# Where the expert tiles run: two batches beside attention, or one stage between the two layers

## The reference

```python
x = x + tanh(g_xattn[0]) * L0_xattn(ctx, layernorm(x), mask, ...)   # 8 heads of 64
x = x + tanh(g_ffn[0])   * L0_ffn(layernorm(x), gate_w, w1, w2, w3) # 8 experts, top 2
x = x + tanh(g_xattn[1]) * L1_xattn(ctx, layernorm(x), mask, ...)   # 16 heads of 64
x = x + tanh(g_ffn[1])   * L1_ffn(layernorm(x), w1, conv_w, conv_b, w2)
...
y   = w2[e] @ (silu(w1[e] @ t) * (w3[e] @ t))      # for each of a token's two experts
out = sum of y over the two experts, weighted by the sparse mixer of their logits
```

## Time and profile before

| what | us |
|---|---|
| median of three runs | 1522.95 |
| the three runs | 1511.71 to 1533.22 |
| the profiled execution | 1511.2 |
| its span, first to last instruction | 1509.4 |

### The profile page before, as it was taken

One profiled execution on the slowest core, in us unless ns is written; L12 is line 12 of the kernel. 1 busy time (PEld: TensorE's weight loads), 2 busy tenths in 40 slices (PEclk: granted clock), 3 DMA queues, 4 the chain that ended last, 5 costly groups with the idle time before them and its releaser, 6 DMA issues.

```text
span 1509.4 us, 45217 instructions
## 1 busy us (share of the span) xinstructions
PE 1266.7 (84%) x16918; PEld 992.1 (66%) x16918; DVE 1055.9 (70%) x2830; ACT 973.3 (64%) x2319; POOL 1112.8 (74%) x1359
## 2 busy tenths in 40 slices
PE   1777788668879889868999999999999999999952
PEld 1445566447658767646888888677777777776742
DVE  4778788976556556775666666678878778777744
ACT  2678787455446566645656565777778777787831
POOL 5778888696567675457676777788888988888764
PEclk9999999889989999989999999999999999999965
DMA  9599998495998974448999998455455456355520
GB/s 313 138 204 237 252 237 186 75 232 141 249 204 235 230 161 84 95 98 196 240 247 255 251 261 221 93 102 107 92 98 101 100 103 106 87 104 99 79 41 7
DMA packets 438329, 239.96 MB, mean 159 GB/s; under 512 B 388848, under 2 KB 420320, under 8 KB 429024
## 3 DMA queue, kind: packets, MB, share of 16 engines
q1 hardware_dynamic: 408216, 178.51, 57.6%
q10 hardware_dynamic: 26824, 51.22, 11.2%
q0 software_dynamic: 3072, 7.34, 1.8%
HBM read 107.78 MB, written 35.50 MB: 95 GB/s over the span
## 4 chain that ended last, share of the span: by engine, by line
PE 23%; POOL 17%; ACT 16%; DMA 12%; DVE 12%; issue 9%; DVEq 4%; SPq 3%; ACTq 3%; POOLq 0%
POOL probs L649 5%; PE bank_ring L1128 5%; DMA probs_turned<-probs 5%; DMA expert_up<-experts_up 5%; ACT scores L844 4%; PE bank_ring L1090 4%; ACT probs L851 4%; DVE scores L1344 4%; PE bank_ring L1076 3%; PE bank_ring L1143 2%; DMA context<-in_ctx 2%; ACTq L987 2%; ACT keys L864 2%; ACT values L871 2%; PE bank_out L1109 2%
## 5 line engine op out<-in xcount | busy, mean ns | idle before, releaser
L649 POOL TENSOR_TENSOR probs<-scores,probs 112x487 f16<-112x487 f32 x384 | 424.9, 1123 | 207.7 <-ACT probs L851 202.1
L844 ACT ACTIVATE scores<-scores,score_min 112x487 f32<-112x487 f32 x384 | 265.9, 694 | 146.0 <-DVE score_min L1344 144.4
L1361 DVE SCALAR_TENSOR_TENSOR values<-bank_ring,values 128x512 f16<-128x512 f32 x192 | 132.4, 690 | 207.8 <-ACT values L871 207.3
L1344 DVE CUSTOM_DVE_ANT_0 scores<-bank_scores,mask 112x487 f32<-112x487 f32 x384 | 238.2, 657 | 1.8 <-PE bank_scores L1049 1.8
L851 ACT ACTIVATE probs<-scores 112x487 f16<-112x487 f32 x384 | 214.6, 604 | 33.0 <-DMA probs_turned<-probs 17.7
L1090 PE MATMUL bank_ring<-weights,kv_B 128*128 128x128 f16 x3072 | 194.9, 220 | 0.9 <-DVE raw_weights L1639 0.6
L1090 PEld LDWEIGHTS bank_ring<-weights,kv_B 128*128 128x128 f16 x3072 | 183.2, 99 | 11.5 <-DVE raw_weights L1639 0.9
L1109 PE MATMUL bank_out<-values,probs_turned 128*128 128x64 f16 x4608 | 170.4, 194 | 23.3 <-DMA probs_turned<-probs 20.8
L1076 PE MATMUL bank_ring<-kv_B,weights 128*128 128x488 f16 x768 | 181.9, 373 | 9.3 <-DVE keys L1356 9.2
L871 ACT ACTIVATE values<-bank_ring 128x512 f16<-128x512 f32 x192 | 112.2, 584 | 100.4 <-PE bank_out L1109 96.3
L1109 PEld LDWEIGHTS bank_out<-values,probs_turned 128*128 128x128 f16 x4608 | 157.2, 99 | 28.0 <-DMA probs_turned<-probs 14.1
(11 more groups left out here) (230 smaller groups left out, 2479.4 us busy)
## 6 DMA issues: line engine op xcount, KB each, us to landing
expert_up<-experts_up SPq DMA_DIRECT2D x43, 1024.0 KB, 5.3
expert_down<-experts_down SPq DMA_DIRECT2D x43, 512.0 KB, 6.8
raw_weights<-in_weights ACTq DMA_DIRECT2D x8, 1536.0 KB, 11.1
experts_up<-expert_up ACTq DMA_DIRECT2D x8, 1024.0 KB, 5.0
raw_weights<-in_weights ACTq DMA_DIRECT2D x6, 1024.0 KB, 8.9
probs_turned<-probs SPq DMA_TRANSPOSE x384
context_turned_B<-kv_B ACTq DMA_DIRECT2D x16, 375.0 KB, 8.5
kv_B<-context_turned_B ACTq DMA_DIRECT2D x16, 375.0 KB, 3.7
```

The source lines that it names most:

```text
L649: pool.tensor_tensor(PR[:, u % 4, 1, 0:KEYS], S[:, u % 4, 0:KEYS], PR[:, u % 4, 0, 0:KEYS], ALU.subtract).then_inc(probs_split, 1)
L844: act_e.activation(S[:, u % 4, 0:KEYS], S[:, u % 4, 0:KEYS], ACT.Exp, bias=rmin[:, u % 4:u % 4 + 1], scale=-1.0, accum_out=rsum[:, g % 2, ...
L1344: dve.tensor_tensor_reduce(out=S[:, u % 4, 0:KEYS], in0=bS[u % 2][0:TOK, 0:KEYS], in1=mask[:, m, 0:KEYS], scale=1.0, scalar=3.0e38, op0=AL ...
L1361: dve.scalar_tensor_tensor(vN[:, j % 2, 1].rearrange("p t d -> p (t d)"), bank("v", j)[:], 1 / WSCALE, vN[:, j % 2, 0].rearrange("p t d -> ...
```

## The change

The steps of layer B no longer follow those of layer A: `pair(s)` maps steps 0 to 63 to layer A and steps from `B_STEP` = 120 to layer B. Between them, from `FIRST_TILE` = 75, one stage runs all tiles, one a step. Routing goes in four groups of sequences (0 to 4, 5 to 9, 10 to 13, 14 and 15); the state `room`, `end` and `pages` carries over from group to group, so a group's rows first fill what is free on an expert's last page and then open new ones. As all groups share pages, there are at most 35 tiles. Each group's choices follow its last sequence, and its rows are scattered two a step; experts and weights of the choices are worked out once, from step 77. Rows of a tile are loaded plainly and turned by PE (`turn_rows`, four transposes) and copied by ACT (`copy_rows`), not by a DMA transpose; weights have three buffers, the third in the place of layer A's attention weights; `down` of a tile runs two steps behind its `up`. Expert chunks are prepared one a step, steps 1 to 48; the FFN weights are summed and rounded from steps 52 and 58 on, layer B's weights split from step 67. The diff, cut:

```diff
 PAIRS = A_STEPS + 8 * NSEQ
-FIRST_STEP, LAST_STEP = -9, PAIRS + 21
+
+
+GROUPS = ((0, 5), (5, 10), (10, 14), (14, 16))
+TILES = (2 * TOK * NSEQ + EXPERTS * 127) // 128
+SCATTERS = 2
+XR_SLOTS = 8
+ZERO_DMAS = -(-TILES // XR_SLOTS)
+
+
+def slack(g):
+    return 0 if g == NSEQ - 1 else 1
+
+
+def routed(b):
+    n = GROUPS[b][1] - 1
+    return 4 * n + 10 + slack(n)
+
+
+FIRST_TILE = routed(len(GROUPS) - 1) + 5
+DOWN_LAG = 2
+B_STEP = FIRST_TILE + TILES + DOWN_LAG + 8
+FIRST_STEP, LAST_STEP = -9, B_STEP + 8 * NSEQ + 21
 PT_BUFS = 5
 
 
-BATCHES = ((0, 6), (6, 16))
-TILES = tuple((2 * TOK * (b - a) + EXPERTS * 127) // 128 for a, b in BATCHES)
-SCATTERS = (3, 4)
-XR_SLOTS = 10
-ZERO_DMAS = sum(-(-t // XR_SLOTS) for t in TILES)
-
-
-def is_pair(j):
-    return 0 <= j < PAIRS
+def pair(s):
+
+    if 0 <= s < A_STEPS:
+        return s
+    return s - B_STEP + A_STEPS if B_STEP <= s < B_STEP + PAIRS - A_STEPS else None
+
+
...
-def first_tile_step(b):
-    return routed(b) + 4 + -(-len(scatters(b)) // SCATTERS[b])
-
-
-def tile(b, i):
-    return i + (TILES[0] if b else 0)
-
...
+def tile_up(s):
+    i = s - FIRST_TILE
+    return i if 0 <= i < TILES else None
+
+
+def tile_turn(s):
+    return tile_up(s + 1)
+
+
+def tile_down(s):
+    return tile_up(s - DOWN_LAG)
 
...
 
 EXPERT_STEP = 1
-WSUM_STEP = 31
-FFN_SUM_STEP, FFN_STEP = 26, 32
-L1_STEP = 41
+FFN_SUM_STEP, WSUM_STEP, FFN_STEP = 52, 57, 58
+L1_STEP = FFN_STEP + 9
+WEIGH_STEP = FIRST_TILE + 2
 
 
 def expert_chunks(j):
-    i = 2 * (j - EXPERT_STEP)
-    return range(i, i + 2) if 0 <= i < EXPERTS * MOE_CHUNKS else range(0)
+    i = j - EXPERT_STEP
+    return range(i, i + 1) if 0 <= i < EXPERTS * MOE_CHUNKS else range(0)
...
         if is_pair(j):
-            uses.append(("v", j))
-        if m[1]:
-            uses.append(m[1])
+            uses.append(("v", pair(j)))
+        if tile_up(j) is not None:
+            uses.append(("up", tile_up(j), 1))
+        if tile_down(j) is not None:
+            uses.append(("down", tile_down(j)))
         uses += late(j)
-        if m[2]:
-            uses.append(m[2])
     return uses
...
+        ctx_flat = ctxb[:].rearrange("p a t d -> p (a t d)")
+        aT = ctx_flat.bitcast(F16).rearrange("p (b a m t) -> p b a m t", b=3, a=2, m=EB)
+        tile_ups = [eup[:, 0], eup[:, 1], W[:, 0:UP_WORDS]]
+        tile_downs = [edown[:, 0], edown[:, 1], W[:, UP_WORDS:UP_WORDS + DOWN_WORDS]]
...
+            def load_rows(t):
+                if t == 0:
+                    for b in range(len(GROUPS)):
+                        sp.wait_ge(scattered[b], 16 * len(scatters(b)))
                 if t >= 2:
-                    sp.wait_ge(up_ready, 2 * (t - 2) + 2)
-                sp.dma_start_transpose(xT[:, t % 2], xs[b][128 * i:128 * i + 128, :])\
-                    .then_inc(xt_loaded[t % 2], 16)
...
+            def load_up(t):
+                if t == 0:
+                    sp.wait_ge(slots_ready, len(GROUPS))
                     sp.wait_ge(ex_stored[0], 32 * 4)
                     sp.wait_ge(ex_stored[1], 32 * 4)
-                e = sp.value_load(ids[b][0:1, i:i + 1], min_val=0, max_val=EXPERTS - 1)
-                if part == 0:
-                    if t >= 2:
-                        sp.wait_ge(up_ready, 2 * (t - 2) + 2)
...
-                else:
-                    if t >= 2:
-                        sp.wait_ge(down_ready, t - 1)
-                    sp.dma_start(edown[:, t % 2], down_dram[e]).then_inc(down_loaded[t % 2], 16)
-
-            def store_result(b, i):
...
+            def load_down(t):
+                e = sp.value_load(ids[0:1, t:t + 1], min_val=0, max_val=EXPERTS - 1)
+                if t >= 3:
+                    sp.wait_ge(down_ready, t - 2)
+                sp.dma_start(tile_downs[t % 3], down_dram[e]).then_inc(down_loaded[t % 3], 16)
+
+            def store_result(t):
                 sp.wait_ge(down_copied, t + 1)
-                sp.dma_start(ys[b][128 * i:128 * i + 128, :], yo[:, t % 2]).then_inc(y_stored[t % 2], 16)
...
-                        load_expert(b, i + 1, 0)
-                    if 2 <= i < TILES[b]:
-                        load_expert(b, i, 1)
+                if j == FIRST_TILE - 2:
+                    load_up(0)
+                    load_down(0)
+                    load_rows(0)
+                    load_rows(1)
+                    for t in (1, 2):
+                        load_up(t)
+                        load_down(t)
+                i = tile_up(j)
+                if i is not None:
+                    if i + 2 < TILES:
+                        load_rows(i + 2)
+                    if i + 3 < TILES:
+                        load_up(i + 3)
+                if 2 <= j - FIRST_TILE and j - FIRST_TILE + 1 < TILES:
+                    load_down(j - FIRST_TILE + 1)
+                if tile_down(j) is not None:
+                    store_result(tile_down(j))
                 for n in range(NSEQ):
...
                         scatter(b, n, k)
+                if tile_up(j) is not None:
+                    split_hidden(tile_up(j), 0)
...
+            def copy_rows(t):
+                act_e.wait_ge(rows_turned, t + 1)
+                if t >= 2:
+                    act_e.wait_ge(up_ready, 2 * (t - 2) + 2)
+                act_e.activation(xT[:, t % 2], bank("rows", t)[:].bitcast(F16)[:, 0:512]
+                                 .rearrange("p (k t) -> p k t", k=4), ACT.Copy).then_inc(rows_copied, 1)
+
...
+            def turn_rows(t):
+                ring_free("rows", t)
+                pe.wait_ge(rows_loaded[t % 2], 16 * (t // 2 + 1))
+                bT = bank("rows", t)[:].bitcast(F16)
+                for q in range(4):
+                    last = pe.transpose(bT[:, 128 * q:128 * q + 128], rows_in[:, t % 2, 128 * q:128 * q + 128], idh[:])
+                last.then_inc(rows_turned, 1)
...
-                m = micro(j)
-                expert(m[0])
+                    proj_q(p)
+                    proj_k(p)
+                if tile_up(j) is not None:
+                    up(tile_up(j), 0)
+                if tile_turn(j) is not None:
+                    turn_rows(tile_turn(j))
                 for t in early(j):
                     part(t)
                 if is_pair(j):
-                    proj_v(j)
-                expert(m[1])
+                    proj_v(pair(j))
+                if tile_up(j) is not None:
+                    up(tile_up(j), 1)
+                if tile_down(j) is not None:
+                    down(tile_down(j))
                 if is_pair(j - 2):
-                    sum_values(j - 2)
...
+            def choose_slots(b, i):
+                n0, n1 = GROUPS[b]
                 nb = n1 - n0
                 lg = LG[:, n0:n1]
...
                 src, top, place = (t2 if i else lg), rv[:, i], rv[:, 2 + i]
                 dve.tensor_reduce(top[:, 0:nb], src, AX.X, ALU.max)
                 dve.drain()
                 dve.tensor_tensor(t1, src, spread(top, nb), ALU.is_equal)
-                dve.tensor_tensor(ex, lg, spread(top, nb), ALU.subtract)
-                dve.scalar_tensor_tensor(keep, lg, -1.0, spread(top, nb), ALU.mult, ALU.max)
                 dve.drain()
                 dve.tensor_tensor(t1, t1, every, ALU.mult)
-                dve.tensor_scalar(ex, ex, 0.0, None, ALU.min)
-                dve.tensor_tensor(keep, keep, lg, ALU.max)
                 dve.drain()
                 dve.tensor_reduce(place[:, 0:nb], t1, AX.X, ALU.max)
-                last = dve.scalar_tensor_tensor(keep, keep, JITTER, ex, ALU.mult, ALU.add)
-                if i:
-                    last.then_inc(route_shifted, 1)
                 dve.drain()
                 dve.tensor_tensor(one[i], t1, spread(place, nb), ALU.is_equal)
...
-                n0, n1 = BATCHES[b]
-                nb, nt = n1 - n0, TILES[b]
+                n0, n1 = GROUPS[b]
+                nb = n1 - n0
                 t1, t2 = rt["t1"][:, 0:nb], rt["t2"][:, 0:nb]
...
                 dve.wait_ge(side_filled, SIDE_AT[("route", b)])
-                dve.tensor_copy(t1, bX[0:TOK, 0:nb * EXPERTS].rearrange("p (n e) -> p n e", e=EXPERTS))
...
+                dve.tensor_scalar(tmp, new, ROUND, None, ALU.add)
+                dve.drain()
+                dve.tensor_scalar(new, tmp, ROUND, None, ALU.subtract)
+                dve.drain()
+                dve.tensor_tensor(c8[:], lower[:],
+                                  new.rearrange("p (o e) -> p o e", o=1).to_broadcast([128, EXPERTS, EXPERTS]),
                                   ALU.mult)
...
-                dve.tensor_tensor(t1, t1, each[0:TOK].rearrange("p (o e) -> p o e", o=1)
-                                  .to_broadcast([TOK, nb, EXPERTS]), ALU.add)
-                dve.tensor_tensor(cmp_[:, 0:nt],
-                                  tile_no[:, 0:nt].rearrange("p (t o) -> p t o", o=1).to_broadcast([128, nt, EXPERTS]),
-                                  ends.rearrange("p (o e) -> p o e", o=1).to_broadcast([128, nt, EXPERTS]),
```

(43 more changed lines are left out.)

411 lines of the change are left out of this document (194 added, 217 removed).

## The result

The changed kernel takes 1570.22 us (1559.89 to 1579.49, four runs), the kernel before on the same chip 1528.09 us (1511.71 to 1536.81, four runs): a ratio of 1.031, 95% interval 1.019 to 1.043. It is slower, by 1.9 to 4.3%, about the 42 us between the medians; forecast was no change, 1530 us in a range from 1495 to 1570. The profiled execution took 1571.77 us with a span of 1570.0 us.

What follows compares the result with a forecast made beforehand. It took PE to bound layer B and no engine alone layer A. Terms 50.9 + 443.2 + 233.5 + 726.6 + 62.6 = 1516.8 us, 7.4 above the 1509.4 span; added to the 1522.95 median, 1530, range 1495 to 1570.

Steps and rivals of the forecast that it cites:

- a tile takes 4.7 us: Stage between the layers: each tile 4.7 us, between bounds of 4.3 and 5.9; 35 tiles make 164.5 us.
- Both lower bounds: Tiles of the stage: PE's work 4.3 us a tile; transport of 1.84 MB at 427 GB/s also 4.3 us.
- the new waits: Stage: SP's first rows wait for scatters, PE's turn of rows for their load, POOL's first gather for the last store.
- rival 1: Stage: tiles wait for their weights, 5.9 us a tile, +42 us, 1572 us; chance 0.26 with whatever else lengthens the stage.
- 8 us of waits for transposes in layer A: Layer A: waits like the 9.74 us one come with expert loads and stores, whose number stays; 8 in all.
- The forecast's own sign: Layer A: the forecast is wrong if a step leaves 5.7 to 7.1 us.
- 6.4 us a step: Layer A, steps 0 to 55: one chunk a step gives 6.4 us each, 358.4 us in all.
- two routings at 13: Layer A: two groups of five sequences routed inside its steps, 13 us extra each, 26 in all.
- Entry: Start of the stage, before the tiles: 40 us, plus 5 for the third group's place_rows ahead of norm_out.
- exit with the last downs: End of the stage: 4 us for the last two downs and 20 us from result copy to first mask.
- 37 us for eight tiles fewer: Whole kernel: 35 tiles instead of 43 earn 37 us of some 199 if nothing else moved.
- Rival 3: Whole kernel: nothing fuses, stage and layers cancel within 2%; this is the forecast itself, chance 0.58.

Runs made afterwards that it cites:

- e_noload: The changed kernel without the loads of the weights of experts 2 to 7, stores kept: 1549.78 us, one execution.
- the four traces: Traces with the same layer A code: the changed kernel, e_rows, e_rows_half, and the changed kernel with 6 of 35 tiles run; layer A 458.7 to 472.7 us.
- e_groups3: The changed kernel with three groups of sequences instead of four and three scatters a step instead of two: 1557.81 us, ratio 1.024 to the kernel before.
- b_35: The kernel before with 15 and 20 tiles run instead of 18 and 25, all result stores kept: 1482.83 us, one execution.
- b_few: The kernel before with 2 + 2 of its 43 tiles run, all result stores kept: 1351.09 us.
- the repaired forms: Three versions of the changed kernel with early rows, chunkwise expert weights and three groups, differing in groups, scatters and result buffers: each at ratio 0.997 to the kernel before.
- e_rows: The changed kernel with a tile's rows loaded six tiles ahead instead of two: 1531.76 us, ratio 1.013 to the kernel before.
- e_rows_half: e_rows with only half of each weight load made from tile 3 on: 1520.9 us in one execution.
- e_all2: The changed kernel with early rows, chunkwise expert weights, groups of 7, 6 and 3 sequences and two scatters a step: 1507.71 us, ratio 0.997 to the kernel before.

## Why the prediction was wrong

**Forecast: a tile takes 4.7 us. Measured: a pitch of 5.61, and 193.5 us where the term had 164.5.** This is the largest error, 29 us. Both lower bounds were nearly right: PE's 4.3 is 4.21 measured, and with early rows, where the transport holds the tiles, its 4.3 by the earlier trace rows has become 4.48. The step that failed is "Two loops of equal length never mesh fully; I take 4.7". There were not two loops but a chain through both, from one load of rows to another, and it has its own length, 11.0 us for two tiles: 4.2 of work and issues, and 6.8 for a load that is asked for behind 1.5 MB. The forecast had this wait in its hand twice. Under the new waits it names PE's turn of the rows, with `up` and `down` behind, and gives it no time; and rival 1 names the queue, with a chance of 0.26 together with whatever else lengthens the stage. That rival 1's 1572 us are close to the 1570 measured is partly luck: it put all 42 us on the tiles, at 5.9 us for lack of bandwidth. The bandwidth was there, the tiles brought 29 us, and layer A, which it left as forecast, 22.

The Trainium skill's 358 GB/s a core ("DMA: Bandwidth & Descriptors", Specifications) would have made an estimated 5.1 us a tile. The stage with early rows moved 405 GB/s, of which 1.70 of every 1.84 MB, 374 GB/s, are reads. The measurement decides against it as a limit here. The Trainium skill's 81 ns for each weight load and matmul ("TensorE: Matmul & The Clock Gate", Back-to-back issue gap) would have added an estimated 1.2 us to PE's part of a tile, 5.5 in all. It is 4.21.

**Forecast: 8 us of waits for transposes in layer A. Measured: 19 to 33 us hang on the loads of expert weights** (e_noload against the four traces; 26.0 against the changed kernel's). The term was sized from the single wait of 9.74 us in the earlier trace rows, with the argument that the number of loads stays. What failed is that step: the number stayed, but where a load, a store and a context's spill came together one or two transposes held all for 10 to 28 us. The forecast's own sign showed it, a step of layer A above 7.1 us: steps 8 to 23 took 7.6. The rest of layer A was right: 6.4 us a step (6.26 in e_noload); two routings at 13 (steps 27 to 30 take 38.0 us and 47 to 50 39.1, 12.4 and 13.5 over 6.4 each); the last eight steps 46.2 against 50.8. Some 9 us of steps 0 to 55 (419.4 less 358.4, 25.9 and 26.0) went away in no run; in e_noload 4.6 of them are step 33. Nor was one chunk a step the relief that the forecast took it for: without tiles, layer A is as long in the one form as in the other.

**Entry 47.6 against 45, exit with the last downs 26.9 against 24.** Near, but the third group's routing on DVE delays norm_out by 7.1 us (e_groups3) where place_rows had been given 5.

**Layer B 723.9 against 726.6, tail 62.6.** Right.

**37 us for eight tiles fewer.** Right in size: 28.4 to 34.4 us in b_35. A tile beside attention costs 4.1 to 4.3 us rather than the 4.6 of 199/43.

**Why the change loses,** all by the spans of the traces: eight tiles fewer at the 4.1 us of b_few -33; the other 35 at 5.53 us in the stage (193.5/35) instead of 4.1, +50; entry and exit +74.5 (47.6 + 26.9), in which PE works 21 us; the two layers without tiles -30 (1252.1 us with the tail, against b_few's 1298.4 less four tiles at 4.1), most of it the second batch's routing; the head -1. Together some +61 us, against 60.6 between the spans (1570.0 and 1509.4) and 42 between the medians. The sum has to close, because the 4.1 is what b_few leaves of the kernel before; what it shows is the size of the parts. Rival 3's idea that stage and layers cancel was nearly true of the repaired forms, where the +50 becomes +12 (155.3/35 = 4.44 us), and entry and layer A give some of the rest.

## What to carry to other kernels

The tiles' time was that of a closed chain through engines and queues, not the larger of their loads and their work. Before taking a mean of two bounds, follow one small transfer from its issue to the instruction that needs it, and count the bytes ahead of it on its queue. Work that fills gaps beside other work gains nothing by a stage of its own unless it runs faster there than it cost in the gaps: here a tile cost 4.1 to 4.3 us beside attention and 4.21 at best alone, and then entry and exit were to be paid. And the size of a wait found once in a trace is not its mean: look at every step that has the same neighbours.

## What the runs showed of the hardware

- A DMA share is not a rate. The tiles stood at a share of 0.92 with 325 GB/s in the changed kernel and at 1.01 with 405 GB/s in e_rows, with the same transfers in another order. With half of each weight load (e_rows_half) the share was 0.83 at 262 GB/s.
- A load of 131 KB landed in 2.1 us where it came first, and in 6.8 us at the median of all 35, most of which stood behind 1.5 MB on their queue.
- The transposes of probs, in packets of 256 bytes, are held up by something well below full rate: in e_all2 such packets took 22 ns on average at 98 to 102 us, where the core moved 205 GB/s, and 70 ns at 92 to 96 us, where it moved 112 and ACT's queue carried pieces of weights and the end of a context's spill in packets of 750 bytes. One transpose took 11.4 us on the chain there. Which neighbour did it was not separated.
